# Two heads' score products in one block at the head of every second step

## What is computed

```python
x = x + tanh(g_xattn[0]) * L0_xattn(layernorm(x), ctx_2048, ...)   # 16 heads of 128, RMS norms, softmax
x = x + tanh(g_ffn[0])   * L0_ffn(layernorm(x), ...)               # base product, 2 of 8 LoRA experts
x = x + tanh(g_xattn[1]) * L1_xattn(layernorm(x), ctx_2048, ctx_2048)  # sigmoid attention, no weights
x = x + tanh(g_ffn[1])   * L1_ffn(layernorm(x), ...)               # 1 of 8 experts
```

```python
q = rms_norm(x @ q_w + q_b, nq_s).reshape(B, S, H, D)         # H = 16, D = 128
k_img = rms_norm(img_ctx @ ki_w + ki_b, nki_s).reshape(B, -1, H, D)
v_img = (img_ctx @ vi_w + vi_b).reshape(B, -1, H, D)
out = sdpa(q, k_img, v_img).reshape(B, S, INNER) @ o_w + o_b
```

## Time and profile before

| | |
|---|---|
| median of 3 runs | 1357.01 us (1357.0 to 1357.02) |
| the profiled execution's own time | 1356.92 us |
| its span, first to last instruction | 1355.1 us |
| TensorE busy | 1326.7 us (98%) |
| VectorE, ScalarE busy | 767.6 us, 765.8 us (57% each) |
| one steady group on TensorE | 160.30 us |
| mean granted TensorE clock | 0.997 of full |

### The profile page before, as it was taken

One profiled execution on the slowest core, in us unless ns is written; L12 is line 12 of the kernel. 1 busy time (PEld: TensorE's weight loads), 2 busy tenths in 40 slices (PEclk: granted clock), 3 DMA queues, 4 the chain that ended last, 5 costly groups with the idle time before them and its releaser, 6 DMA issues.

```text
span 1355.1 us, 26606 instructions
## 1 busy us (share of the span) xinstructions
PE 1326.7 (98%) x10367; PEld 1155.5 (85%) x10367; DVE 767.6 (57%) x2315; ACT 765.8 (57%) x2092; POOL 74.1 (5%) x114
## 2 busy tenths in 40 slices
PE   7899999999999999999999999999999999999998
PEld 6788888988898788988889888998889888888777
DVE  7644555546555464665555465564656555554575
ACT  4375666566465574756556565556646556466522
POOL 3000000010000000000000100001000000001010
PEclk9999999999999999999999999999999999999999
DMA  8312522224122321222212231122312112122100
GB/s 303 110 63 79 141 94 68 75 63 125 48 70 64 102 94 47 63 94 79 94 47 71 70 125 63 47 79 82 110 44 79 63 63 94 48 78 65 62 1 32
DMA packets 51451, 108.47 MB, mean 80 GB/s; under 512 B 8224, under 2 KB 32000, under 8 KB 50688
## 3 DMA queue, kind: packets, MB, share of 16 engines
q1 hardware_dynamic: 51328, 106.77, 24.3%
HBM read 89.98 MB, written 16.78 MB: 79 GB/s over the span
## 4 chain that ended last, share of the span: by engine, by line
PE 86%; DVE 10%; ACT 3%; issue 1%; DMA 0%; SPq 0%; DVEq 0%
PE bank L114 57%; PE bank L1053 8%; PE bank L1063 5%; PE bank L1024 3%; PE bank L1042 3%; PE bank L1163 2%; PE bank L1175 2%; PE bank L1205 1%; PE bank L1014 1%; PE bank L1117 1%; ACT xn L785 1%; PE bank L994 1%; DVE rstd L80 1%; DVE logit L1534 1%; DVE ao_lo L1525 1%
## 5 line engine op out<-in xcount | busy, mean ns | idle before, releaser
L114 PE MATMUL bank<-sv,ct_hi 128*128 128x256 f32 x1024 | 195.7, 289 | 0.0
L114 PE MATMUL bank<-so,ao_hi 128*128 128x256 f32 x1016 | 188.2, 284 | 0.3 <-DVE ao_lo L1525 0.3
L1525 DVE SCALAR_TENSOR_TENSOR ao_lo<-bank,vecs,ao_hi 128x512 fp32r<-128x512 f32 x127 | 95.3, 751 | 159.7 <-ACT ao_hi L754 158.9
L760 ACT ACTIVATE expo<-logit,least 128x64 f32<-128x64 f32 x512 | 171.6, 337 | 20.6 <-DVE least L1536 20.6
L754 ACT ACTIVATE ao_hi<-bank,vecs 128x512 fp32r<-128x512 f32 x127 | 87.0, 685 | 155.0 <-PE bank L1053 154.5
L114 PEld LDWEIGHTS bank<-so,ao_hi 128*128 128x128 f32 x1016 | 162.4, 189 | 8.5 <-issue 0.5
L114 PEld LDWEIGHTS bank<-sv,ct_hi 128*128 128x128 f32 x1024 | 156.6, 189 | 0.1
L1534 DVE TENSOR_TENSOR logit<-bank,rr 128x256 f32<-128x256 f32 x128 | 54.4, 425 | 162.4 <-PE bank L1063 161.9
L779 ACT ACTIVATE q_sb<-bank,qbias,qscale 128x512 f32<-128x512 f32 x128 | 99.3, 776 | 80.3 <-PE bank L114 79.8
L114 PE MATMUL bank<-sv,ct_lo 128*128 128x256 f32 x512 | 143.1, 279 | 0.0
L114 PE MATMUL bank<-so,ao_lo 128*128 128x256 f32 x508 | 142.3, 280 | 0.0
(11 more groups left out here) (239 smaller groups left out, 2668.0 us busy)
## 6 DMA issues: line engine op xcount, KB each, us to landing
sv<-v_scratch SPq DMA_DIRECT2D x56, 512.0 KB, 3.4
so<-o_scratch SPq DMA_DIRECT2D x56, 512.0 KB, 3.3
xin<-in_x_dram SPq DMA_DIRECT2D x8, 512.0 KB, 4.8
cin<-in_ctx_dram SPq DMA_DIRECT2D x32, 128.0 KB, 4.8
xres<-in_x_dram SPq DMA_DIRECT2D x8, 512.0 KB, 4.7
c_scratch<-cs SPq DMA_DIRECT2D x8, 512.0 KB, 5.0
v_scratch<-sv SPq DMA_DIRECT2D x8, 512.0 KB, 3.1
o_scratch<-so SPq DMA_DIRECT2D x8, 512.0 KB, 2.6
```

The lines of the kernel that those rows point to most:

```text
L114: last = pe.matmul(out, lhs[a], rhs[b], start=start and n == 0, stop=stop and n == 2, **kw)
L760: last = act.activation(expo[:, t, :], logit[:, t, :], ACT.Exp, scale=-1.0, bias=least[:, t:t + 1], accum_out=rsum[:, t:t + 1])
L1525: dve.scalar_tensor_tensor(out=lo[:, :], in0=attention_bank(g, h)[:, :], scalar=vecs[:, v:v + 1], in1=hi[:, :].bitcast(F32), op0=ALU.add, ...
```

## The change

TensorE's step becomes, for even h: `scores(h-2)`, `scores(h-1)`, k(h), a, `attend(h-3)`, b, v(h), c, q(h), `prob_transpose(h-2)`, d, `output(h-3)`, e. Odd steps have no scores (but for the last two heads of the last group). Buffers for q, logits, least and sums are doubled; the exponentials are written over the logits. ScalarE starts a step with `exps(h-2)`, ahead of k's copy. VectorE starts an even step with the logits of both heads, and the shares of point a follow, ahead of `probabilities`. `split(b, 1)` stands behind `attn_lo`, `prob_copy` behind points b and c. `score_factors` goes from (14, c) to (14, d). The tail of the last group is written in another order, and `expert_scale(NEXT)` goes into `end`.

```diff
 PREP_BANKS = 6
-TURN_LAG, ATT_LAG, OUT_LAG = 2, 3, 4
+TURN_LAG, ATT_LAG, OUT_LAG = 2, 3, 3
...
-    least = sb("least", [P, NT])
-    rsum = sb("rsum", [P, NT])
+    least = sb("least", [P, 2, NT])
+    rsum = sb("rsum", [P, 2, NT])
...
-    q_sb = sb("q_sb", [P, GT])
-    logit = sb("logit", [P, NT, SEQ])
-    expo = sb("expo", [P, NT, SEQ])
+    q_sb = sb("q_sb", [P, 2, GT])
+    logit = sb("logit", [P, 2, NT, SEQ])
...
-    gt = sb("gt", [E1, GT])
+    gt = th[0:E1, 0, :, :].rearrange("p c d -> p (c d)")
...
-        return pj_ps[0] if (g, h) == (LAST, H - 2) else pv_ps
+        return {(LAST, H - 2): pj_ps[0], (LAST, H - 1): at_ps}.get((g, h), pv_ps)
...
+                last = act.activation(logit[:, h % 2, t, :], logit[:, h % 2, t, :], ACT.Exp, scale=-1.0, bias=least[:, h % 2, t:t + 1],
+                                      accum_out=rsum[:, h % 2, t:t + 1])
...
         def step(b, h):
             main = live(b, h)
+            final = main and h == H - 1 and not is_body(b, NG - 1)
+            if live(b, h - TURN_LAG):
+                exps(b, h - TURN_LAG)
+            if main:
+                project(b, h, 0)
             share(b, h, "a")
             if live(b, h - ATT_LAG):
                 attn_hi(b, h - ATT_LAG)
+            share(b, h, "b")
             if main:
-                project(b, h, 0)
-            share(b, h, "b")
+                project(b, h, 1)
+                if final:
+                    split_context(b + 1)
+            share(b, h, "c")
+            soon = main and (h % 2 == 1 or (b, h) == (LAST, H - 2))
+            if soon:
+                project(b, h, 2)
             if live(b, h - TURN_LAG):
                 prob_copy(b, h - TURN_LAG)
-            share(b, h, "c")
-            if live(b, h - 1):
-                exps(b, h - 1)
-            if main:
-                project(b, h, 1)
-                if h == H - 1 and not is_body(b, NG - 1):
-                    split_context(b + 1)
+            if main and not soon:
+                project(b, h, 2)
+            if final:
+                split_tokens(b + 1)
             share(b, h, "d")
-            if main:
-                project(b, h, 2)
-                if h == H - 1 and not is_body(b, NG - 1):
-                    split_tokens(b + 1)
             share(b, h, "e")
...
             step(LAST, h)
+        exps(LAST, H - 2)
         exps(LAST, H - 1)
+        prob_copy(LAST, H - 2)
         attn_hi(LAST, H - 3)
-        prob_copy(LAST, H - 2)
+        prob_copy(LAST, H - 1)
+        attn_hi(LAST, H - 2)
+        turned_gates(NEXT)
+        attn_hi(LAST, H - 1)
         expert_exp(NEXT)
-        attn_hi(LAST, H - 2)
-        prob_copy(LAST, H - 1)
-        attn_hi(LAST, H - 1)
         end()
...
         def scores(g, h):
             pe.wait_ge(pj_read.sem, pj_read.count(g, 3 * h + 2))
-            l_ready.wait(pe, g, h - 1)
+            l_ready.wait(pe, g, h - 1 if (g, h) == (LAST, H - 1) else h - 1 - h % 2)
...
-                    last = pe.matmul(at_ps[i * SEQ:(i + 1) * SEQ, t * SEQ:(t + 1) * SEQ],
-                                     q_sb[:, s], k_sb[:, h % 2, keys(t, i)], start=True, stop=True)
+                    last = pe.matmul(at_ps[i * SEQ:(i + 1) * SEQ, (h % 2 * NT + t) * SEQ:(h % 2 * NT + t + 1) * SEQ],
+                                     q_sb[:, h % 2, s], k_sb[:, h % 2, keys(t, i)], start=True, stop=True)
...
         def step(b, h):
             main = live(b, h)
+            if (b, h) == (0, 2):
+                gr_read.wait(pe, 0, 2 * NT - 1)
+            if h % 2 == 0 and live(b, h - 2):
+                scores(b, h - 2)
+                scores(b, h - 1)
+            if (b, h) == (LAST, H - 1):
+                scores(b, h - 1)
+            if main and (b, h) != (0, 0):
+                project(b, h, 0)
+            share(b, h, "a")
+            if live(b, h - ATT_LAG):
+                attend(b, h - ATT_LAG)
+            share(b, h, "b")
+            if main:
+                values(b, h)
+            share(b, h, "c")
+            if (b, h) == (0, 1):
+                norms(-1)
+            if main:
+                project(b, h, 2)
+            if live(b, h - TURN_LAG):
+                prob_transpose(b, h - TURN_LAG)
+            share(b, h, "d")
             if live(b, h - OUT_LAG):
                 output(b, h - OUT_LAG)
-            if live(b, h - ATT_LAG):
-                attend(b, h - ATT_LAG)
-            share(b, h, "a")
-            if main and (b, h) != (0, 0):
-                project(b, h, 0)
-            share(b, h, "b")
-            if (b, h) == (0, 1):
-                norms(-1)
-                gr_read.wait(pe, 0, 2 * NT - 1)
-            if live(b, h - 1):
-                scores(b, h - 1)
-            if live(b, h - TURN_LAG):
-                prob_transpose(b, h - TURN_LAG)
-            share(b, h, "c")
-            if main:
-                values(b, h)
-            share(b, h, "d")
-            if main:
-                project(b, h, 2)
+            if (b, h) == (LAST, H - 1):
+                scores(b, h)
             share(b, h, "e")
...
-        scores(LAST, H - 1)
-        gate_logits(NEXT)
-        output(LAST, H - 4)
+        turned_gates(NEXT)
+        prob_transpose(LAST, H - 2)
         attend(LAST, H - 3)
-        prob_transpose(LAST, H - 2)
+        prob_transpose(LAST, H - 1)
         attend(LAST, H - 2)
-        prob_transpose(LAST, H - 1)
         output(LAST, H - 3)
         attend(LAST, H - 1)
+        gate_logits(NEXT)
         output(LAST, H - 2)
         output(LAST, H - 1)
...
-            dve.wait_ge(qk_full.sem, qk_full.count(g, h))
+            dve.wait_ge(qk_full.sem, qk_full.count(g, h if (g, h) == (LAST, H - 2) else h + 1 - h % 2))
...
-                if at == (14, "c"):
+                if at == (14, "d"):
                     score_factors(n)
...
         def step(b, h):
-            if h == 0 and not is_body(b, 0) and live(b, 0):
+            first = h == 0 and not is_body(b, 0) and live(b, 0)
+            if first:
                 split(b, 0)
+            if h % 2 == 0 and live(b, h - 2):
+                logits(b, h - 2)
+                logits(b, h - 1)
+            if (b, h) == (LAST, H - 1):
+                logits(b, h - 1)
+            share(b, h, "a")
             if live(b, h - TURN_LAG):
                 probabilities(b, h - TURN_LAG)
-            if h == 0 and not is_body(b, 0) and live(b, 0):
-                split(b, 1)
-            share(b, h, "a")
             if live(b, h - ATT_LAG):
                 attn_lo(b, h - ATT_LAG)
-            if is_body(b, 0) and h == 1:
+            if first:
+                split(b, 1)
+            if (b, h) == (0, 1):
                 score_factors(0)
-            if live(b, h - 1):
-                logits(b, h - 1)
+            share(b, h, "b")
+            share(b, h, "c")
             if live(b, h - TURN_LAG):
                 prob_copy(b, h - TURN_LAG)
-            share(b, h, "b")
-            share(b, h, "c")
             share(b, h, "d")
             share(b, h, "e")
...
+            expert_scale(NEXT)
```

More of the change, by code:

```diff
@@ L487, in attention_bank @@
     def attention_bank(g, h):
-        return pj_ps[0] if (g, h) == (LAST, H - 2) else pv_ps
+        return {(LAST, H - 2): pj_ps[0], (LAST, H - 1): at_ps}.get((g, h), pv_ps)
     def attention_parts(g, h):
-        return [v["k"][:, 0, 0:GT] for v in (w_hi, w_lo)] if (g, h) == (LAST, H - 2) else [ao_hi, ao_lo]
+        own = g == LAST and h >= H - 2
+        return [v["k"][:, h - (H - 2), 0:GT] for v in (w_hi, w_lo)] if own else [ao_hi, ao_lo]
     def turned_probs(g, h, t):
@@ L765, in prob_copy @@
             act.wait_ge(pt_full.sem, pt_full.count(g, h))
+            if g == LAST and h >= H - 2:
+                act.wait_ge(pv_full.sem, pv_full.count(g, h - 1))
             act.activation(pt_part(0), turned_probs(g, h, 0), ACT.Copy).then_inc(pt_ready[0].sem, 1)
@@ L778, in project @@
             else:
-                act.activation(q_sb[:, :], bank[:, :], ACT.Identity, scale=qscale[:, h:h + 1],
+                act.activation(q_sb[:, h % 2, :], bank[:, :], ACT.Identity, scale=qscale[:, h:h + 1],
                                bias=qbias[:, h:h + 1]).then_inc(pj_read.sem, 1)
@@ L1037, in prob_transpose @@
                 pj_read.wait(pe, g, 3 * H - 2)
+            elif (g, h) == (LAST, H - 1):
+                l_ready.wait(pe, g, h)
             else:
-                ao_ready.wait(pe, g, h - 2 if (g, h) == (LAST, H - 1) else h - 1)
+                ao_ready.wait(pe, g, h - 1)
             bank = attention_bank(g, h)
@@ L1518, in prob_copy @@
             dve.wait_ge(pt_full.sem, pt_full.count(g, h))
+            if g == LAST and h >= H - 2:
+                dve.wait_ge(pv_full.sem, pv_full.count(g, h - 1))
             dve.tensor_copy(pt_part(1), turned_probs(g, h, 1)).then_inc(pt_ready[1].sem, 1)
@@ L1529, in logits @@
         def logits(g, h):
[L1531 removed]
+            dve.wait_ge(qk_full.sem, qk_full.count(g, h if (g, h) == (LAST, H - 2) else h + 1 - h % 2))
```

(23 more changed lines are left out.)

11 lines of the change are left out of this document (2 added, 9 removed).

## The result

The changed kernel takes 1364.11 us (median of 5 runs, 1362.51 to 1365.07) against 1357.0 in the same comparison: a ratio of 1.0053, with a 95% interval of 1.0041 to 1.0064. That is 7.1 us slower, more than the 0.2% bound. Forecast were 1362.5 and "slower" with 0.53. The profiled execution took 1364.54, its span 1362.7.

What follows compares the result with a forecast made beforehand. TensorE's own stream was taken to bound a group, 159.56 of 160.30 us busy. Nine terms summed to +5.8 on 1356.92, giving 1362.7, stated as 1362.5, with a range of 1348 to 1370.

Steps and rivals of the forecast that it cites:

- Terms 1 and 2: TensorE's stream: fewer array-shape switches, -11.9 us; waits that go because their places move behind q or from their writer, -7.5.
- Term 3: Kernel start: TensorE's 3.0 stop for `v_sb` and the half clock go, smaller waits come: -3.2 us, ends 0 and -5.
- Term 4: Step 0 of groups 1 to 7: q newly waits for `xt_lo`, 1.6 in six groups, 1.9 in group 1: +11.5 us.
- Term 5: Step 2: head 0's transpositions wait for `ao_lo` behind `expert_scale` and variances, 1.1 to 1.2 in five groups: +5.9 us.
- Term 6: Group 0 and small ones: late transpositions at steps 4, 6, 12; late weights wait 1.4 more for `rr`: +4.5 us.
- Term 7: Steps 6 and 15: k's copy some 0.1 late behind a normalisation on ScalarE: +1.4 us, ends 0 and 4.
- Term 8: The tail: loses three short stops and gains others: 0 us, ends -3 and +3.
- Term 9: The clock: the new step 0 waits bring three falls to half clock in seven: +5.1 us, ends 0 and 12.
- The rival without falls: No falls of the clock at the new step 0 waits: sum +0.7, 1357.6 us, no change; chance 0.20.
- The faster rival: Chain from scores to `xt_lo` and `ao_lo` shorter than counted, step 0's wait about 0.9: -7.5, 1349.4 us; chance 0.27.
- The marks set ahead: Profile signs: x32 blocks about 1.1, seven `xt_lo` waits, five `ao_lo` waits, steady group 160 to 163, over three half-clock stretches.

## Why the prediction was right, and where it wasn't

The sum said +5.8 and +7.1 was measured. It is right in its sign and its size. Two terms failed (7 and 9), in opposite directions, and two more (6 and 8) are right in their sums but not in their parts.

- **Terms 1 and 2** (switches, waits that go): -2.3 a steady group was forecast (1.4 and 0.9), -2.3 measured (162.00 without its stops against 160.30). The switch was measured by itself at 0.30 a pair of heads, forecast 0.26. How the 2.3 divides between the two terms was not measured.
- **Term 3** (start, -3.2, end -5): TensorE's fourth q starts 4.6 earlier than before (67.64 against 72.23), of which 0.3 or so belongs to term 1. That is 1.1 more than the -3.2, and inside its ends. The fall of the clock there went, as forecast.
- **Term 4** (+11.5): 6 x 1.43 + 1.57 = +10.2, in the seven places named. Undoing its cause alone gave back 9.8.
- **Term 5** (+5.9): 5 x 1.20 = +6.0. Undoing its cause gave back 5.7.
- **Term 6** (+4.5): between the fourth q and group 1's first, 3.7 were lost, where terms 1, 2, 4 and 6 gave -2.1 - 0.9 + 1.9 + 4.5 = +3.4. The stop for `rr` became 2.9, forecast 3.0. But the agreement of this term is in part luck: the three late transpositions cost 0.45, 0.45 and 0.55 and not 0.6, 1.2 and 1.2, while the wait of group 1's first k for `ct_lo`, which no term has, grew from 0.51 to 1.96, because VectorE is still at the late weights (`b1t_lo`).
- **Term 7** (+1.4, ends 0 and 4) is the step that failed: "In steps 6 and 15 k's copy comes some 0.1 late behind a normalisation". At step 6 the stop is 1.37 in six groups, +8.2. The nine Newton instructions stand between logits and probabilities. At 0.16 each they leave TensorE without a stop, as the run with GpSimd's additions cut shows; at 0.67 for four of them they cost 1.37. In the kernel before the same additions hit `shift` alone. I had moved the instructions with the durations of their old neighbours.
- **Term 8** (0): from the last q to the end 78.6 pass in both kernels. But the last group, in which TensorE has no wait on the list at steps 2 and 6, takes 143.75 from its first q to its last instead of 144.49: terms 1 and 2 give 0.7 there and not 2.3, and why was not read.
- **Term 9** (+5.1, ends 0 and 12) failed as "three falls in seven": none of seven stops of 1.4 was followed by one. It stands at its lower end. The prediction placed the limit between 0.96 and 1.62; the last section shows that a length doesn't decide. The rival without falls had the clock right; what it lacked is the step 6 stop, 6.8.

Terms 7 and 9 were off by +6.8 and -5.1, so that the total is nearer than its parts, and that is luck: a range that holds the time does not show that its reasons held. From q to q the whole difference is accounted for: -4.6 at the fourth q, +3.7 to group 1's first, +0.7 over group 1, 5 x 1.7 over the next five, -0.7 for the rest make 7.6, as between the two profiled executions. The faster rival is out: its chain would have made step 0's stop 0.9, and it is 1.43. The marks set ahead were met for the block (x32, 1.08), for `xt_lo` (seven, 1.27 to 1.4), for five of the `ao_lo` waits and for the group (162.00 in 160 to 163). The six further `ao_lo` waits and the count of half-clock stretches were not.

## What to carry to other kernels

Where two heads' work is joined into one block, the chain behind it (logits, exponentials, probabilities, low part) gets longer and meets whatever stands ahead of it on VectorE's queue. Walk that queue step by step and put everything that TensorE doesn't wait for behind the instruction that it does wait for: here that, with the score factors' place in group 0, turned a loss of 7 us into a gain of 21. When an instruction moves, look again at what the other engines do beside its new place, and don't carry its duration over.
